# Softmax denominators of an attention block: fewer GpSimd additions, more TensorE column sums, seven probability buffers, and scratch tensors laid out by tile

## The reference, cut to what matters

```
q = rope(layernorm(x));  k = rope(ctx);  v = ctx
scores = q k^T / sqrt(32) + slope_h * (key - query)
x = x + tanh(g0) * softmax(scores) v
x = x + tanh(g1) * ffn(layernorm(x))
```

## Time and profile before

| | |
|---|---|
| median of three runs | 1798.62 us |
| the profiled execution's own time | 1800.73 us |
| its span, first to last instruction | 1798.9 us |
| granted clock of TensorE, mean over the span | 0.965 |
| attention, about 55 to 905 us | PE busy 818 of 850 us |
| GpSimd in 600 to 800 us | busy 200.00 of 200 us |
| product stage, 1440 to 1547 us | PE busy 4.67 of 107 us |

### The profile page before, as it was taken

One profiled execution on the slowest core, in us unless ns is written; L12 is line 12 of the kernel. 1 busy time (PEld: TensorE's weight loads), 2 busy tenths in 40 slices (PEclk: granted clock), 3 DMA queues, 4 the chain that ended last, 5 costly groups with the idle time before them and its releaser, 6 DMA issues. The chain is left out here.

```text
span 1798.9 us, 36886 instructions
## 1 busy us (share of the span) xinstructions
PE 1605.8 (89%) x14777; PEld 633.3 (35%) x14777; DVE 1479.7 (82%) x2116; ACT 1241.8 (69%) x1974; POOL 838.6 (47%) x504
## 2 busy tenths in 40 slices
PE   3899999999999999999869999999999900699999
PEld 0233333333333333333224444444444400344444
DVE  7899999999998898898569989768889998854551
ACT  3688888888889899888723323359986699844440
POOL 5699999999999999998600100200000000000000
PEclk9999999999999999999979999999999955899999
DMA  6688888988888887776649888569973479755551
GB/s 153 151 154 179 167 164 180 177 164 167 163 173 161 171 183 151 163 151 136 139 117 275 242 250 239 203 194 284 280 226 127 139 250 302 237 189 172 176 168 61
DMA packets 344204, 331.73 MB, mean 184 GB/s; under 512 B 214849, under 2 KB 273601, under 8 KB 336097
## 3 DMA queue, kind: packets, MB, share of 16 engines
q1 hardware_dynamic: 335104, 264.37, 55.2%
q0 software_dynamic: 8928, 65.02, 18.3%
HBM read 136.77 MB, written 76.55 MB: 119 GB/s over the span
## 5 line engine op out<-in xcount | busy, mean ns | idle before, releaser
L1348 DVE TENSOR_REDUCE cm<-quad 128x1 f16<-128x1024 f32 x512 | 600.3, 1214 | 63.3 <-PE quad L921 62.3
L1145 ACT ACTIVATE P<-quad 128x512 f32<-128x512 f32 x1024 | 556.8, 598 | 112.3 <-PE quad L934 100.5
L1936 POOL TENSOR_TENSOR Ps<-P,P 128x2048 f32<-128x2048 f32 x93 | 441.0, 4742 | 43.2 <-ACT P L1145 43.1
L934 PE MATMUL quad<-QA,KA 101*32 101x512 f16 x4096 | 365.9, 385 | 6.8 <-ACT P L1145 5.3
L921 PE MATMUL quad<-KA,QA 100*32 100x512 f16 x4096 | 334.7, 391 | 35.6 <-DMA QA<-S 17.8
L983 PE MATMUL quad<-P,cg 128*32 128x512 f32 x2048 | 265.5, 594 | 0.0
L1010 PE MATMUL quad<-x_hl,Wu 128*128 128x512 f16 x1152 | 250.8, 381 | 3.4 <-DMA Wu<-wt_scratch 3.4
L1010 PE MATMUL quad<-x_hl,Wg 128*128 128x512 f16 x1152 | 249.3, 379 | 3.1 <-DMA x_hl<-xs 2.5
L1063 PE MATMUL quad<-Wd,oh 128*128 128x512 f16 x768 | 228.6, 379 | 0.0
L934 PEld LDWEIGHTS quad<-QA,KA 101*32 101x32 f16 x4096 | 105.0, 94 | 298.6 <-ACT P L1145 231.0
L1226 ACT ACTIVATE ev<-quad 128x1024 f32<-128x1024 f32 x96 | 97.3, 1014 | 123.4 <-PE quad L1010 117.3
(11 more groups left out here) (167 smaller groups left out, 2006.3 us busy)
## 6 DMA issues: line engine op xcount, KB each, us to landing
Ps<-P POOLq DMA_DIRECT2D x62, 1024.0 KB, 8.1
gate_scratch<-ev SPq DMA_DIRECT2D x48, 512.0 KB, 3.8
gt<-gate_scratch SPq DMA_DIRECT2D x48, 512.0 KB, 5.8
up_scratch<-ev SPq DMA_DIRECT2D x48, 512.0 KB, 3.4
uf<-up_scratch SPq DMA_DIRECT2D x48, 512.0 KB, 5.1
uf<-up_scratch SPq DMA_DIRECT2D x96, 256.0 KB, 3.6
wt_scratch<-wh SPq DMA_DIRECT2D x72, 128.0 KB, 2.8
xl<-in_x_dram SPq DMA_DIRECT2D x32, 256.0 KB, 5.1
```

The source lines that it names most:

```text
L934: mm = e.matmul(K.score[h % 2][j:j + 32, :], K.KA[p % 2][0:101, kt, h, j:j + 32], K.QA[p % 2][0:101, 4 * qc:4 * qc + 4, h, :], start=True, ...
L1145: e.activation(K.Pb[pb][:, h, :], K.score[h % 2], ACT.Exp, scale=SCALE / (QPOW * KPOW)).then_inc(K.a_exp, 1)
L1348: e.tensor_reduce(cm[:, col:col + 1], K.quad[UNIT["max", hm, u] % 2][:, :], AX.X, ALU.max).then_inc(K.v_max, 1)
L1936: e.tensor_tensor(K.Ps[n][:, :, :], K.Pb[(st.g - 1) % NP][:, :, :], K.Pb[st.g % NP][:, :, :], ALU.add).then_inc(K.g_sum, 1)
```

## The change

- GpSimd no longer adds tiles 6 and 7. It adds tiles 0 and 1 into `Ps0` and tiles 3 and 4 into `Ps1`; the two DMAs add tiles 2 and 5 to them as before. `Ps2` is gone.
- PE makes four denominator groups for a half: `Ps0` in step 6, tile 6 itself in step 7, tile 7 itself in step 0 of the next half, and `Ps1` in step 2. All four stand behind PV. Step 1 has none. This holds for the 31 halves before the last.
- There are seven probability buffers (`NP` = 7); the seventh lies where `Ps2` was.
- `gate_scratch` and `up_scratch` are (12, 4, 128, 1024): the 512 KB of a tile are contiguous. The DMAs move the same bytes between the same buffers, in the same order.

```diff
-NXL, NWL, NWQ, NP = 7, 4, 2, 6
+NXL, NWL, NWQ, NP = 7, 4, 2, 7
...
-        self.sum = (hf, s // 2) if last and s % 2 == 1 else (hf, {1: 0, 4: 2, 7: 1}[s]) if inside and s % 3 == 1 else None
+        self.sum = (hf, s // 2) if last and s % 2 == 1 else (hf, s // 4) if inside and s in (1, 4) else None
...
-        if s == 6 and inside:
-            self.dens = (hf, 0)
-        elif s in (1, 2) and 1 <= hf < NHALF:
-            self.dens = (hf - 1, s)
+        if s in (6, 7) and inside:
+            self.dens = (hf, s - 6)
+        elif s in (0, 2) and 1 <= hf < NHALF:
+            self.dens = (hf - 1, 2 + s // 2)
...
-        self.gate_d = nc.dram_tensor("gate_scratch", (OT, 128, N), F32).ap()
-        self.up_d = nc.dram_tensor("up_scratch", (OT, 128, N), F32).ap()
+        self.gate_d = nc.dram_tensor("gate_scratch", (OT, N // GW, 128, GW), F32).ap()
+        self.up_d = nc.dram_tensor("up_scratch", (OT, N // GW, 128, GW), F32).ap()
...
-            if n == 1:
-                e.wait_ge(K.g_sum, sum_no(hf, n))
-            else:
-                e.wait_ge(K.d_acc[n // 2], 16 * hf + 16)
+            src = K.Ps[n % 2]
+        elif n in (1, 2):
+            e.wait_ge(K.a_exp, score_no(hf, n + 5, 3))
+            src = K.Pb[(8 * hf + n + 5) % NP]
+        else:
+            e.wait_ge(K.d_acc[n // 3], 16 * hf + 16)
+            src = K.Ps[n // 3]
         for h in range(4):
-            mm = e.matmul(K.den[32 * h:32 * h + 32, :], K.ones[:, :], K.Ps[n % 2 if hf == NHALF - 1 else n][:, h, :], start=n == 0, stop=n == (3 if hf == NHALF - 1 else 2))
+            mm = e.matmul(K.den[32 * h:32 * h + 32, :], K.ones[:, :], src[:, h, :], start=n == 0, stop=n == 3)
...
-            if hm < NHALF - 1 and km % 3 < 2:
-                e.wait_ge(K.g_sum, 3 * hm + km // 3 + 1)
+            if hm < NHALF - 1 and km >= 6:
+                e.wait_ge(K.pe_den, den_no(hm, km - 5))
+            elif hm < NHALF - 1 and km % 3 < 2:
+                e.wait_ge(K.g_sum, sum_no(hm, km // 3))
...
-        e.dma_start(K.uf[n % NUF][:, 0:w], K.up_d[ot, :, sl]).then_inc(K.d_uf[n % NUF], 16)
+        e.dma_start(K.uf[n % NUF][:, 0:w], K.up_d[ot, cp, :, sl]).then_inc(K.d_uf[n % NUF], 16)
```

More of the change, by code:

```diff
@@ L264, in den_no, with low_no @@
 def den_no(hf, n):
-    return 3 * hf + n + 1
+    return 4 * hf + n + 1
 def sum_no(hf, n):
-    return 3 * hf + (1, 3, 2)[n]
+    return 2 * hf + n + 1
+def low_no(p, w, half):
+    return part_no(p - 1, w, half)
 def rope_no(p, w):
@@ L387, in __init__ @@
         self.KA = [A(f"KA{i}", [128, 8, 4, 128], F16) for i in range(2)]
-        self.Pb = [A(f"P{i}", [128, 4, 512], F32) for i in range(NP - 1)]
+        self.Pb = [A(f"P{i}", [128, 4, 512], F32) for i in range(5)]
         self.bias = nc.alloc_sbuf_tensor_at("bias", [32, T], F32, offset=A.at - 2 * 8192)
         self.biasT = A("biasT", [128, 8, 4, 16], F16)
-        self.Ps = [A(f"Ps{i}", [128, 4, 512], F32) for i in range(3)]
+        self.Ps = [A(f"Ps{i}", [128, 4, 512], F32) for i in range(2)]
+        P6 = A("P6", [128, 4, 512], F32)
         self.numT = A("numT", [128, 512], F32)
@@ L423, in __init__ @@
         self.cg.append(A("cg3", [128, 8, 128], F32))
-        self.Pb.append(A("P5", [128, 4, 512], F32))
+        self.Pb += [A("P5", [128, 4, 512], F32), P6]
         self.xl2 = [A(f"xl2{i}", [128, H], F32) for i in range(2)]
@@ L783, in store_projection @@
         e.wait_ge(K.a_ev, k + 1)
-        e.dma_start(dst_d[ot, :, 1024 * cp:1024 * cp + 1024], K.ev[k % NEV][:, :]).then_inc(K.d_ev[k % NEV], 16)
+        e.dma_start(dst_d[ot, cp, :, :], K.ev[k % NEV][:, :]).then_inc(K.d_ev[k % NEV], 16)
     def load_wu(ot):
@@ L821, in load_gate @@
             e.wait_ge(K.a_gq, n - NGT + 1)
-        e.dma_start(K.gt[n % NGT][:, :], K.gate_d[ot, :, GW * cp:GW * cp + GW]).then_inc(K.d_gt[n % NGT], 16)
+        e.dma_start(K.gt[n % NGT][:, :], K.gate_d[ot, cp, :, :]).then_inc(K.d_gt[n % NGT], 16)
     def load_wd(part, j):
@@ L847, in sync_program, with load_up @@
     uf_uses = [0]
-    def load_up(ot, sl, w):
+    def load_up(ot, cp, sl, w):
         n = uf_uses[0]
@@ L856, in load_up @@
                 e.wait_ge(K.a_uq, n - NUF - 48 + 1)
-        e.dma_start(K.uf[n % NUF][:, 0:w], K.up_d[ot, :, sl]).then_inc(K.d_uf[n % NUF], 16)
+        e.dma_start(K.uf[n % NUF][:, 0:w], K.up_d[ot, cp, :, sl]).then_inc(K.d_uf[n % NUF], 16)
     def load_product(n):
-        load_up(n // 4, slice(GW * (n % 4), GW * (n % 4) + GW), GW)
+        load_up(n // 4, n % 4, slice(0, GW), GW)
     def load_o(n):
         ch, ot = TODO[n]
-        load_up(ot, slice(512 * ch, 512 * ch + 512), 512)
+        load_up(ot, ch // 2, slice(512 * (ch % 2), 512 * (ch % 2) + 512), 512)
     def load_xr(n):
@@ L1178, in scalar_program @@
             hf = st.den_out
-            e.wait_ge(K.pe_den, den_no(hf, 3 if hf == NHALF - 1 else 2))
+            e.wait_ge(K.pe_den, den_no(hf, 3))
             if hf > 0:
@@ L1541, in vector_program @@
             e.wait_ge(K.a_exp, score_no(st.hf, st.s, 3))
-            e.wait_ge(K.pe_den, den_no(st.hf - 1, n) if n < 2 else den_no(st.hf, n - 2))
+            e.wait_ge(K.pe_den, den_no(st.hf - 1, 3 * n) if n < 2 else den_no(st.hf, n - 2))
             e.tensor_tensor(K.Ps[n % 2][:, :, :], K.Pb[(st.g - 1) % NP][:, :, :], K.Pb[st.g % NP][:, :, :], ALU.add).then_inc(K.v_sum, 1)
@@ L1913, in gpsimd_program @@
             e.wait_ge(K.a_exp, score_no(hf, kt, 3))
-            e.wait_ge(K.g_sum, sum_no(hf, 2 * n))
-            e.dma_start(K.Ps[2 * n][:, :, :], K.Pb[(8 * hf + kt) % NP][:, :, :], accum_op=ALU.add).then_inc(K.d_acc[n], 16)
+            e.wait_ge(K.g_sum, sum_no(hf, n))
+            e.dma_start(K.Ps[n][:, :, :], K.Pb[(8 * hf + kt) % NP][:, :, :], accum_op=ALU.add).then_inc(K.d_acc[n], 16)
         if st.rope is not None:
@@ L1934, in gpsimd_program @@
             if hf > 0:
-                e.wait_ge(K.pe_den, den_no(hf - 1, n))
+                e.wait_ge(K.pe_den, den_no(hf - 1, 3 * n))
             e.tensor_tensor(K.Ps[n][:, :, :], K.Pb[(st.g - 1) % NP][:, :, :], K.Pb[st.g % NP][:, :, :], ALU.add).then_inc(K.g_sum, 1)
```

## The result

| | before | changed |
|---|---|---|
| median of four runs | 1799.38 us | 1811.09 us |
| lowest, highest | 1795.56, 1801.59 | 1809.93, 1813.40 |
| profiled execution, its own time | 1800.73 | 1809.93 |
| its span | 1798.9 | 1808.1 |

The changed kernel is slower: the ratio is 1.0066, with a 95% interval of 1.0053 to 1.0079. The forecast was 1806.3 us, or +7.7; measured were +11.7 at the medians and +9.2 between the two profiled executions. The direction and the range held. The sum hides more than it shows, though: in the profile the +9.2 is the difference of two larger parts of opposite sign, each of them further from its forecast than the sum is.

What follows compares the result with a forecast made beforehand. PE was taken to set attention's steps and the up stage, DVE and ACT the product stage. Attention +8.7 and layout -1 made +7.7 on the median 1798.62, about 1806.3 us; 8-in-10 range 1793 to 1818.

Steps and rivals of the forecast that it cites:

- Step 7 gets a group: Attention, step 7: tile 6's group makes PE set the step, 2.95 to 3.53 us, +0.58 a half.
- Step 0: Attention, step 0: tile 7's group lengthens it from 3.03 to 3.53 us, +0.50, and the 0.25 wait for DVE goes.
- Step 1: Attention, step 1: without its group PV waits for numT; the step falls from 3.71 to 3.01 us, -0.70.
- Step 2: Attention, step 2: ACT comes late, so the third score waits for an exponent's bank, +0.46 us a half.
- Lateness: Attention: the mean half's 0.68 us over a clean half mostly goes, 0.12 kept, -0.56 a half.
- Sum for attention: All of attention: 31 x (0.84 - 0.56) = +8.7 us.
- The stores and the loads of gate tiles: Gate and up stages: these transfers lie beside PE's work, so their length changes nothing there.
- I take -1 us: Product stage: gain taken for the scratch layout, between 0 and 5 to 8 us at most.
- The pitch: Scratch loads: by the skill's rule a 16 KB row pitch costs nothing, layout worth 0; by the trace's 0.7 us, 5 us.
- the layout pays: Product stage: waits go, -6 us in place of -1; with attention at +5 to +8.7, 1800 us; chance 0.2.
- first rival: Attention, step 2: ACT absorbs numT, the 0.46 goes, attention is -5.6 us and the time 1792; chance 0.14.

Runs made afterwards that it cites:

- Experiment 6: Changed kernel with DVE's three statistics jobs one step later (steps 7, 0 and 1 in place of 6, 7 and 0): 1812.74 us, ratio 1.0071.
- experiment 7: Changed kernel with ACT's copy and DVE's low part moved from step 6 to step 7 of each half: 1807.02 us, ratio 1.0048.
- Experiment 5: Changed kernel with tile 7's denominator group in step 1 ahead of PV, not in step 0: 1792.69 us, ratio 0.9957 of before.
- experiment 3: Kernel before with only the gate scratch, its store and its load contiguous by tile: 1794.93 us, ratio 0.9978.
- experiment 8: Kernel before, old layout, step 1 taking the sum of tiles 3, 4 and 5, step 2 that of 6 and 7: 1809.94 us, ratio 1.0058.

## Why the prediction was right or wrong, point by point

- *"Step 7 gets a group ... PE's work is 3.53, DVE's 3.02, so PE sets it: 2.95 to 3.53, +0.58."* Wrong; this is the step that failed. It usually lasts 3.80, and over 31 halves step 7 grew by 26.8 us, 0.86 a half, where 0.58 makes 18.0: the group hid nothing there and cost its full length. I compared two sums of work and took the larger, and I put DVE's hold down to its maxima and a statistics job. But the 0.28 that PE lost in step 7 before was a wait for a bank in the middle of the step, ahead of the place of the new group. A group hides a wait only if it stands between what starts the awaited work and the wait. Experiment 6 rules out the statistics, and experiment 7 names the bank: the low part's.
- *"Step 0 ... 3.53"*: right, and for the reason given. The wait in step 0 was behind the group in step 7, so that group did cover it. Experiment 5 shows it pure: step 0 at 2.67.
- *"Step 1 ... ends at +3.01"*, with PE waiting for numT: right (3.04).
- *"Step 2 ... ACT comes late into it: +0.46"*: right (usually 3.95 or 4.01, +0.42 or +0.48); experiment 5 removes it by lengthening step 1.
- *Lateness, -0.56 of 0.68 a half.* Right in size. Steps 1 and 6, where it sat, fell by 38.5 us over 31 halves; -0.70 and -0.56 make 39.1. The usual steps of the changed kernel add up to 27.12 us, the mean half of pairs 3 to 13 is 27.26, so 0.14 is left where I kept 0.12. The cause is in part argued: PE's waits for POOL's sums are gone, but no run separates them from what the longer steps 7 and 0 give DVE.
- Sum for attention: 31 x (0.84 + 0.28 - 0.53) = 18.3, as measured for the 31 halves (18.5 with the last), against 8.7 forecast. Nearly all of the miss, 8.8 of 9.8 us, is step 7.
- *"The stores and the loads of gate tiles lie beside PE's work ... so their length changes nothing there."* Wrong. They share SP's queue with the loads of up weights. SP issues a gate load only when ACT has freed a buffer, and ACT waits for the gate load before; so slow gate loads push the weight loads behind them late, and PE waited for these: at 1309 and 1331 us two starts lie 1.3 and 2.8 us apart in place of 0.22, 3.7 us lost. The second of these before, on SP and on PE:

```profile
1325.45 2.04 SPq L822 DMA_DIRECT2D gt<-gate_scratch  x2
1327.55 2.56 SPq L795 DMA_TRANSPOSE Wu<-wt_scratch  x2
```

```profile
1333.84 8.34 PE L1010 MATMUL quad<-x_hl,Wu 128*128 128x512 f16 x30 [2.45 <-DMA Wu<-wt_scratch]
```

That the wait goes with the gate scratch's layout is shown (experiment 3); that the place in the queue passes it on is argued from these rows, and no run moved the weight loads ahead. The row for it, "DMA Wu<-wt_scratch 3.4" beside the up projections, was on the page, and I read past it. The wait also cost clock: in 1334 to 1338 us before, the granted clock (the third number from the end of the row below) was 0.58 on average, between its levels 1.0 (2.4 GHz) and 0.5 (1.2 GHz), and seven distances between PE's starts are 0.43 us there and two more above 0.22. That is another 1.7 us, and together the 5.4.

```profile
1334.00:1338.00 4.00, 4.00 (x12) 1.50 (x11) 3.67 (x7) 3.97 (x5) 0.00 (x0) 0.58 0.15 58
```

- *"I take -1 us"* for the product stage: 3.0 in the profile. The bound of 5 to 8 us held; the value was too near zero.
- *The pitch.* The Trainium skill's row on the HBM row pitch ("DMA: Bandwidth & Descriptors", section "Latency and other measured facts") tells of losses from 2 MiB on, and of full rate at 512 KiB. Here the pitch was 16 KB, and making the tiles contiguous took the median gate load from 5.8 to 5.2 us and gave 8 us in all. The measurement decides: for these tiles, with 4 KB of a row each, something is to be had well below that pitch. It isn't so for every load: the 256 KB pieces of the down stage, of which a row is 2 KB, land after 3.7 to 4.3 us (medians) with the contiguous up scratch and after 3.6 to 3.7 with the old one, and the down stage stays at 248.4 to 248.7 us. What in the memory makes the difference, no run here shows.
- The 1806.3 came within 5 us of 1811.1 because +9.8 in attention that I missed met -7.4 behind it. That is luck: with either error alone the forecast would have been off by more. The rival "the layout pays" put -6 on the product stage; there it was -3.0, and the other -5.4 came from the up stage, which it didn't name. Its attention part (+5 to +8.7) was too low, so its time of 1800 was wrong as well.
- The first rival's turning point is misstated: attention's +8.7 is gone when 0.28 of the 0.46 a half *doesn't* show up (31 x 0.28 = 8.7), so when 0.18 is left. All of it showed up, so nothing hung on this.

## What to carry to other kernels

Work added to an in-order engine hides the waits that come after it, never those ahead of it in the same step: ask where a wait stands before taking the larger of two sums of work. Moving one denominator group from step 0 to step 1, where it covers another engine's copy, gave back 18 us, all that the change had cost attention. Taking an addition off GpSimd in each half gave back no more, in the placement of experiment 5, than the group that it put on TensorE cost. A transfer that is "hidden beside compute" may still stand in a queue ahead of one that is not: look at who else is issued from there. And price the parts of a change each by itself: the kernel with the layout alone was 19 us faster than the one with both parts.

## What the runs showed of the hardware that was not expected

- Contiguous 512 KB tiles in HBM against rows of 4 KB at a 16 KB pitch: median issue to landing of the gate loads 5.2 us against 5.8, of the up loads in 1430 to 1560 us 4.0 against 4.8 (layout alone against before). Over all thirteen profiles the gate loads' median is 5.1 to 5.3 us with contiguous tiles and 5.7 to 5.8 without.
- After PE had waited 2.6 us in the up stage, its granted clock was 0.58 on average over the next 4 us. With the groups exchanged (experiment 8) it was 0.60 in 1318 to 1322 us, behind a wait of 2.2; with the change in attention alone (experiment 1) a wait of 2.5 us, ended at 1349.8, left it at 1.00. So such a wait costs clock in some executions and not in others.
- GpSimd additions of 128 x 2048 took 4.74 us on average before, with GpSimd busy 782 of 850 us of attention, and 4.58 in the changed kernel (4552 to 4633 ns), with it busy 639.
